# Reordered first and last groups, pairwise adds on GpSimd, and half the state transposes in the last group of a state-space layer kernel

## The reference, cut to what matters

```
x = x + attn(rotate(x))            # rotate: damped rotation of feature pairs, a factor per sequence
x = x + ffn(experts(x))

attn:  xn = layernorm(x)
       for direction in (forward, reverse):
           u, z  = in_proj(xn);  u = silu(causal_conv4(u) + b)        # 256 channels
           dt, B, C = x_proj(u)                                       # 64, 16, 16
           delta = softplus(dt_proj(dt) + b)
           for n in range(16):   h_n = exp(delta*A_n) * h_n[t-1] + delta*u*B_n
           y = sum_n(h_n * C_n) + u*D                                 # 256 channels
           y = y * silu(z);  out_proj
       y = gelu(dim_reduce(both)); y = glu(y) + skip
experts: relu(x Wi_e) Wo_e, low-rank corrected weights of 8 experts, chosen by sequence
ffn:   h = silu(x W1)*(x W2); h = gelu(h H1); h = gelu(h H2); h W3
```

## Time and profile before

| what | value |
|---|---|
| median of 3 runs | 1063.78 us (1063.17 to 1065.88) |
| profiled execution, its own time | 1062.9 us |
| its span, first to last instruction | 1060.6 us |
| PE busy | 943.8 us, 89% |
| DVE busy | 908.4 us, 86% |
| POOL busy | 829.5 us, 78% |
| ACT busy | 778.1 us, 73% |
| chain that ended last | PE 46%, DVE 19%, ACT 17%, issue 15%, POOL 3% |

### The profile page before, as it was taken

How to read it: one execution, slowest core, us unless ns; L and a number is a source line. 1 busy time by engine, 2 the same in 40 slices (tenths; PEclk the granted TensorE clock), 3 DMA queues, 4 the chain that set the end, 5 groups by cost and what they waited for, 6 DMA issues and landing times.

```text
span 1060.6 us, 13662 instructions
## 1 busy us (share of the span) xinstructions
PE 943.8 (89%) x4312; PEld 599.0 (56%) x4312; DVE 908.4 (86%) x718; ACT 778.1 (73%) x1233; POOL 829.5 (78%) x430
## 2 busy tenths in 40 slices
PE   5698678778999899999999999999999988998987
PEld 3455455656655467445755566545755575556455
DVE  1788999999999989999999999998999999968600
ACT  4757667778698768877688868877788758777532
POOL 0767998989988897989878997979878998866300
PEclk9697699898999999999999999999999999999999
DMA  3766675463646555654556554745555465536000
GB/s 95 253 204 208 187 216 180 137 218 116 195 142 194 171 165 147 208 167 144 160 163 183 168 167 123 237 147 168 153 164 187 151 178 146 165 121 169 0 11 6
DMA packets 97670, 167.43 MB, mean 158 GB/s; under 512 B 9920, under 2 KB 33408, under 8 KB 97344
## 3 DMA queue, kind: packets, MB, share of 16 engines
q1 hardware_dynamic: 97600, 166.57, 50.8%
HBM read 159.19 MB, written 7.34 MB: 157 GB/s over the span
## 4 chain that ended last, share of the span: by engine, by line
PE 46%; DVE 19%; ACT 17%; issue 15%; POOL 3%; DMA 0%; DVEq 0%; SPq 0%; POOLq 0%; ACTq 0%
DVE bank_d L905 12%; PE bank_m L1102 9%; PE bank_m L1026 9%; PE bank_y L1190 8%; ACT L586 5%; ACT bank_d L702 5%; PE bank_m L1109 5%; PE bank_m L1116 2%; DVE state L903 2%; PE bank_m L1075 2%; PE bank_m L1084 2%; DVE state L910 2%; POOL state L555 2%; PE bank_m L1044 1%; PE bank_m L1059 1%
## 5 line engine op out<-in xcount | busy, mean ns | idle before, releaser
L555 POOL TENSOR_TENSOR state<-du,b_rows 128x1024 f32<-128x1024 f32 (+1 forms) x288 | 603.9, 2121 | 92.6 <-PE bank_y L1190 91.7
L905 DVE TENSOR_TENSOR_SCAN bank_d<-bank_d,state 128x1024 f32<-128x1024 f32 (+1 forms) x225 | 461.2, 2050 | 44.0 <-ACT bank_d L702 38.6
L702 ACT ACTIVATE bank_d<-delta,a_neg 128x512 f32<-128x512 f32 (+1 forms) x576 | 345.0, 634 | 104.5 <-DVE state L910 94.2
L1190 PEld LDWEIGHTS bank_y<-ident,state 128*128 128x128 f32 x2048 | 240.4, 145 | 81.7 <-issue 55.5
L1190 PE MATMUL bank_y<-ident,state 128*128 128x128 f32 x2048 | 263.3, 281 | 17.8 <-POOL state L560 11.7
L910 DVE TENSOR_TENSOR state<-bank_d,c_rows 128x1024 f32<-128x1024 f32 (+1 forms) x225 | 248.8, 1106 | 7.8
L560 POOL TENSOR_TENSOR state<-state,c_rows 128x1024 f32<-128x1024 f32 (+1 forms) x63 | 134.2, 2131 | 16.4 <-DVE state L903 16.4
L903 DVE TENSOR_TENSOR_SCAN state<-bank_d,state 128x1024 f32<-128x1024 f32 (+1 forms) x63 | 128.7, 2042 | 1.2 <-ACT bank_d L702 1.2
L1109 PE MATMUL bank_m<-hidA,h_s 128*128 128x512 f32 (+1 forms) x256 | 111.8, 584 | 15.6 <-ACT relu_dt L683 9.7
L1026 PE MATMUL bank_m<-xnT,w_conv 128*128 128x508 f32 (+7 forms) x288 | 115.3, 550 | 4.8 <-DVE x1T L930 3.1
L1102 PE MATMUL bank_m<-hidB,h_s 128*128 128x512 f32 (+1 forms) x256 | 110.3, 584 | 1.7 <-DVE hidB L944 0.8
(11 more groups left out here) (143 smaller groups left out, 1011.8 us busy)
## 6 DMA issues: line engine op xcount, KB each, us to landing
b_rows<-bc_store SPq DMA_DIRECT2D x256, 256.0 KB, 4.2
c_rows<-bc_store SPq DMA_DIRECT2D x256, 256.0 KB, 4.3
wsel<-merged SPq DMA_DIRECT2D x32, 512.0 KB, 3.5
merged<-hidA SPq DMA_DIRECT2D x8, 512.0 KB, 3.1
h_s<-in_h SPq DMA_DIRECT2D x2, 1024.0 KB, 8.9
xin<-in_x SPq DMA_DIRECT2D x7, 256.0 KB, 3.9
out<-cT SPq DMA_DIRECT2D x7, 256.0 KB, 3.1
wsel<-in_factors SPq DMA_DIRECT2D x8, 160.0 KB, 3.7
```

The costliest lines, as they stand in the source:

```text
L555: nc.gpsimd.tensor_tensor(split(unit_state(u)), du[:, d, :, :width(g)], per_half(b_rows, u), ALU.mult).then_inc(S.bx_ready, 1)
L702: ins = act.activation(split(unit_decay(u))[:, h], delta[:, d, h, :width(g)], ACT.Exp, scale=a_neg[:, h, n:n + 1])
L905: dve.tensor_tensor_scan(decay, decay, drive, 0.0, ALU.mult, ALU.add).then_inc(S.scanned, 1)
L1190: ins = pe.matmul(bank_y[:, h, s * P:(s + 1) * P], split(unit_state(u))[:, h, s * LEN:(s + 1) * LEN], ident[:, :], start=(n == 0 and s == ...
```

## The change

1. *Tables.* New shifts for the first and last groups, a `SECOND_GROUP` for group 1, and shifts for one of two directions (`"softplus:1"`). In group 0 the forward direction goes first on its own: `norm`, `uf0`, `uf1`, `dbc0`, `dt00`, `dt01`, and only then `ur0`, `ur1`, `z0`, `z1`. Its softplus result is taken by VectorE, not by GpSimd (`first_inputs`). The weights for the convolution are made behind `rotate(0)`, not ahead of it. `u_r` of group 0 gets its Silu in place later. In the last groups `h2_`, `w3` and `tok` of group 7 move behind the last units, between the back fills of group 8.
2. *Pairs.* In group 8 GpSimd adds units n-1 and n for all odd n (`join`, 16 adds of 128x512); TensorE transposes only the sum.
3. *Skip.* In groups 7 and 8 ScalarE writes u*D into `gated`, and TensorE adds it to `bank_y` by transposes ahead of unit 15 in place of the matmuls with `skip`.
4. *Functions.* `h2_` of group 7 is taken with Gelu at once; the sigmoid of group 8 is made with Tanh, which is in the table of Gelu.

```
-        "ur1": -17.5, ... "out": 38.0, ... "h2_2": 65.5
+        "ur1": -19.0, ... "out": 37.5, ... "h2_2": 66.0
...
-TAKE_LAG = {"uf0": 1.5, "uf1": 1.5, "ur0": -6.5, "ur1": 2.0, "dbc0": 0.5, "dbc1": 0.5, "h1_0": 1.5, "h1_1": 0.5,
+TAKE_LAG = {"uf0": 1.5, "uf1": 1.5, "ur0": 1.0, "ur1": 2.5, "dbc0": 0.5, "dbc1": 0.5, "h1_0": 0.5, "h1_1": 0.5,
...
-DIRECT = {"gate": NG - 1, "h1_": NG - 1, "h2_": NG - 1}
+JOINED, JOIN_LAG = (1, 3, 5, 7, 9, 11, 13, 15, 17, 19, 21, 23, 25, 27, 29, 31), 1
+BY_SCALAR = NG - 2
+DIRECT = {"gate": NG - 1, "h1_": NG - 1, "h2_": NG - 2}
...
+            def join(u):
+                wait_product(pool, u - 1)
+                wait_product(pool, u)
+                nc.gpsimd.tensor_tensor(unit_state(u), unit_state(u - 1), unit_state(u), ALU.add).then_inc(S.joined, 1)
...
+            def skip(g, d):
+                wait_u(act, g, d)
+                if g > 0:
+                    wait_filled(act, g - 1, "out")
+                w = width(g)
+                for h in range(HALVES):
+                    ins = act.activation(gated[:, d, h, :w], (u_f, u_r)[d][:, g % 2, h, :w], ACT.Copy, scale=c("skip_d", h))
+                ins.then_inc(S.skipped, 1)
...
+            def first_inputs():
+                w = width(0)
+                dve.wait_ge(S.log_ready, 1)
+                dve.tensor_tensor(delta[:, 0, :, :w], relu_dt[:, :, :w], log_dt[:, :, :w], ALU.add).then_inc(S.delta_ready, 1)
+                dve.wait_ge(S.delta_ready, 1)
+                wait_u(dve, 0, 0)
+                dve.tensor_tensor(du[:, 0, :, :w], delta[:, 0, :, :w], u_f[:, 0, :, :w], ALU.mult).then_inc(S.du_ready, 1)
...
             def sum_states(u):
                 g, d, n = unit(u)
-                wait_product(pe, u)
-                if n == 0:
+                if joined(u + 1):
+                    return
+                first = n - 1 if joined(u) else n
+                if joined(u):
+                    pe.wait_ge(S.joined, sum(u - u % UNITS + k <= u for k in JOINED))
+                else:
+                    wait_product(pe, u)
+                if first == 0:
                     wait(pe, S.gated_ready, 2 * g + d)
+                if n == NST - 1 and g >= BY_SCALAR:
+                    pe.wait_ge(S.skipped, 2 * (g - BY_SCALAR) + d + 1)
+                    for h in range(HALVES):
+                        for s in range(sequences(g)):
+                            pe.matmul(bank_y[:, h, s * P:(s + 1) * P], gated[:, d, h, s * LEN:(s + 1) * LEN], ident[:, :],
+                                      start=False, stop=False, is_transpose=True, skip_group_check=True)
```

115 lines of the change are left out of this document (71 added, 44 removed), and 35 rows, old and new, of tables (FILL, FIRST_GROUP, LAST_GROUP, NEXT_TO_LAST).

## The result

The changed kernel takes 1074.71 us as a median of 5 runs (1071.78 to 1079.20), the kernel before 1063.78 us (1062.82 to 1065.88): a ratio of 1.0101, with a 95% interval of 1.0086 to 1.0117. It is 1% slower, where 1.2% faster was forecast. Its profiled execution took 1079.2 us (span 1075.4), its slowest, so 4.5 us of what that profile shows is not in the median.

The account below looks back on a forecast made before the run. It took VectorE and TensorE as full in wide groups, TensorE as pacing group 8, and the tail as a chain through TensorE. 1062.9 - 4.6 - 0 - 6.4 - 1.8 = 1050.1, or 1051.0 as a median; range 1042 to 1059.5.

Parts of the forecast that it names:

- The start, 4.6 us less: Up to the first scan: reordered first inputs let dbc0 and the first scan start 4.6 us earlier, bounds 4.0 to 5.8.
- Within group 0 ... I take no change: Group 0: VectorE has the same work; its 9.5 us of idle may shrink or grow by 4, taken as no change.
- the start's gain is lost in group 0: Rival: merges and group 1's convolution set group 0's pace, so an earlier first scan only waits more; 1055.6 us, chance 0.11.
- Wide groups, 0: Wide groups: VectorE has the same instructions, so no change, with 5 us either way over the middle.
- That group is VectorE's: Group 7: skip transposes take some 1.5 us off TensorE and add four ScalarE copies, but VectorE limits the group.
- Group 8, 6.4 us less: Group 8: joins and fewer transposes shorten it from 76.9 to 70.5 us, bounds 68.6 to 79.
- Here TensorE sets the pace: Group 8 in the kernel before: TensorE, busy 71.51 of 76.90 us, limits the stretch.
- That GpSimd would become the bound: Group 8: 16 joins add 20.3 us, giving GpSimd 70.2 us with a wait, narrowly above TensorE's 68.6.
- The tail, 1.8 us less: Last product to the end: less skip work and less TensorE idle, 35.9 us in place of 37.78; bounds 0 to 4.5.
- Joins do not hold VectorE: Judges a rival for group 8: each join holds VectorE for its 1.27 us, 10.8 us more, 1061.8 us; chance 0.03.
- GpSimd gives group 8 back: Rival for group 8: GpSimd's waits for scans stay beside the joins, the stretch takes 79 us, total 1059.5; chance 0.13.
- h1_0 a unit earlier: Slower rival, all groups: the earlier take holds up ScalarE's decays, then VectorE, 2.5 us each, 1068.5 us; chance 0.04.

Follow-up runs that it names:

- late_rstd: The changed kernel with GpSimd's rstd of group 1 moved behind the weighing of unit 3, instead of ahead of two drives: 1069.3 us.
- new_front_alone: The changed kernel with rstd of group 1 late, groups 2 to 8 in the order of before, no joins: 1066.3 us.
- old_order_no_joins: The changed kernel's code with every number of order of all groups and merges as before, and no joins: 1063.5 us.
- gap_filler_front: joins_but_last plus three idle products on TensorE in two gaps of group 0: 1069.3 us.
- middle_old_order: The changed kernel with the numbers of order of groups 2 to 6 as before: 1076.4 us.
- before_wide_filler: The kernel before plus one idle TensorE product in each of groups 2 to 7, ahead of the fill dt00: 1064.7 us.
- less_tensor: late_rstd_no_joins with 42 of TensorE's state transposes in group 8 left out and nothing put on GpSimd: 1068.4 us.
- late_rstd_no_joins: The changed kernel with rstd of group 1 late and without any joins: 1070.0 us.
- joins_but_last: The changed kernel with rstd of group 1 late and without the last join, units 30 and 31 summed apart: 1065.7 us.
- tail_filler: The changed kernel with rstd of group 1 late, all joins, and two idle TensorE products ahead of the wait for the last join: 1066.4 us.

## Why the prediction was wrong, point by point

**The start, 4.6 us less: right in this profile (4.75), in part by luck.** I forecast that the convolution starts at 12.3 us and `dbc0` at 19.3. They start at 13.20 and 19.00: the earlier rotation gained nothing, since GpSimd's `rstd` took 1.54 us in place of 0.71, and the 16 records took 5.20 us where I had allowed some 6.5. The other profiles with this front have 5.06 to 6.66 for them. Their first scans stand at 29.7 to 31.3 us (13 profiles, middle value 30.55), those of the old order at 32.6 to 34.65 (7 profiles, 33.37). That makes 2.8 us, under my lower bound of 4.0.

**"Within group 0 ... I take no change": the first failed step.** It went by VectorE's amount of work and its 9.5 us of idle, and did not follow the new order on the three engines around it. Group 0 took 84.35 us in place of 76.09. Where the new order puts `rstd` ahead of a weighing that TensorE's sums need, 5.4 us of the median were lost (shown by late_rstd). Even without that the start's gain does not reach the end: new_front_alone starts 3.8 us earlier than old_order_no_joins, and its time is that of the kernel before (1.0000). This is the rival "the start's gain is lost in group 0", which had 0.11. Its mechanism, that merges and the convolution of group 1 set the pace, fits gap_filler_front but was not tested by itself; that a part is lost later, in the wide groups, was not in it.

**Wide groups, 0: wrong by 8 us in the profile in groups 2 to 6 and by 2.9 in group 7, the cause open.** "That group is VectorE's" did not hold for group 7 in the new order (114.25 to 117.06 us, 114.05 in the old). The numbers of groups 2 to 6 are not what makes these longer (middle_old_order). Nor is it wholly the change's: with the order of before in these groups and in those ahead they took 587.3, 590.6, 589.5 and 591.2 us in four profiles. Falls of TensorE's clock behind 1.1 to 1.4 us of idle go with such differences, and where one was prevented in one place (before_wide_filler) another came elsewhere. The profiles behind the new front lie higher, at 591 to 595; what in the front decides that no run has told.

**Group 8, 6.4 us less: the second failed step.** "Here TensorE sets the pace" was read from 71.51 us busy out of 76.90. less_tensor takes 42 transposes away with nothing put elsewhere, and group 8 stays at 77.0. The 6.4 us became 0.3 in the profile; in pairs of profiles the joins bring 0.5 and 2.0 us, and the scatter from profile to profile is as large. VectorE's waits were already in the earlier trace rows as 10.7 us for ScalarE's decays, the longest 3.95. I put them down to the takes of TensorE's fills without asking what else ScalarE was doing ahead of them; ahead of the longest it is two table loads and a Gelu. That GpSimd would become the bound was wrong as well: it is busy 64.8 of 76.5 us and waits for scans 6.0.

**The tail, 1.8 us less: right in the reordering, wrong on the join.** Without the last join the part behind the last product is 56.4 to 56.5 us, 2.6 to 2.7 less than before, above my 1.8 and within its bounds (57.2 was forecast). I priced the last join at its 1.3 us on the path. It costs 4.3, since TensorE idles 2.77 us for it and goes on at half clock. On the scale of medians it is 3.6. My sum for the tail had no term for the clock.

**The sum.** 1074.7 less 5.4 for `rstd` less 3.6 for the last join is 1065.7, where the kernel before is at 1063.8 to 1064.5: two small decisions make more than four fifths of the loss in the medians (9.0 of 10.9), and what is left (1.0018, 1.0006 to 1.0031) is the rest of the front and of the wide groups against the gain of the tail. Each of the two steps is clear of its interval; their sizes are less sure, since late_rstd_no_joins, without the last join, stands at 1070.0.

**The rivals.** Joins do not hold VectorE: the scans stay at 1222 ns beside 15 adds on GpSimd in the stretch. The rule of the Trainium skill on the shared port ("Perfetto Trace Analysis", Optimizing Scalar/DVE Operations) was rightly given little. Another rule of the Trainium skill ("Perfetto Trace Analysis", Matmul Optimizations) says that matmuls should run back to back in batches, because the engine scales its power with its use. By it, joins_but_last and tail_filler agree (2.9 us of clock at one gap); gap_filler_front shows no gain by it, for there the clock was back at 42 us, group 0 took 78.7 us as in late_rstd (78.8), and the median (1069.3) was no lower than joins_but_last's (1065.7). "GpSimd gives group 8 back" and "h1_0 a unit earlier" did not happen.

No version here beats the kernel before; old_order_no_joins, 1063.5 with a ratio of 0.9972 to 1.0008, is the same as it.

## What to carry to other kernels

When an order is changed, follow each moved instruction that waits on another engine: list what stands behind it in its queue and who needs that, since here a 1 us instruction cost 5 us and a 1.3 us add at the end of a chain 4. An engine that is busy 93% of a stretch need not set its pace: look up the few longest waits of the engine that the work must pass through, and read what their releaser did just before. Idle time of TensorE ahead of a long block of matmuls can cost its length plus the block at half clock (2.77 us and 5.47 in place of 3.60 here), so price both, and compare profiles only with several executions of the same order at hand.

## What the runs showed of the hardware

The granted clock does not follow from the program alone. Behind the same idle time of 1.36 us TensorE ran 8 matmul records in 3.70 us in one group and in 5.40 in the next. With the same order and the same two gaps (2.13 and 3.67 us) it was back at full clock at 48 us in one execution and at 57 in another, though busy without a break from 50. Two idle products of 0.94 us each in a gap of 2.77 us kept it at full clock.
